# The transposed embeddings laid out slot by slot instead of sample by sample, in a DLRM interaction tower on one core

## Chip, cores and metric

One core of one Trainium2 chip. The metric is device time in microseconds of one execution of the kernel. Its engines are named as in the profile: PE (TensorE, with PEld for its weight loads), DVE (VectorE), ACT (ScalarE), POOL (GpSimd), SP (SyncE).

## The reference

For each of 512 samples, 27 embedding rows of 128 numbers are looked up in 27 tables, all pairs of the 27 are multiplied (a dot product each), and the 351 products with 16 dense numbers go through a tower of three layers. All in float32.

```python
e = jnp.stack([tbl_0[ids[:, 0]], ..., tbl_26[ids[:, 26]]], axis=1)   # 512 x 27 x 128
dot_products = jnp.einsum('bnd,bmd->bnm', e, e)
r, c = np.tril_indices(27, k=-1)
z = dot_products[:, c, r]
h = jnp.concatenate([z, dense_ctx], axis=1)                          # 512 x 367
h = jnp.maximum(h @ W_top1 + b_top1, 0.0)                            # 367 x 512
h = jnp.maximum(h @ W_top2 + b_top2, 0.0)                            # 512 x 256
y = h @ W_top3                                                       # 256 x 1
```

## The kernel before

**Tiling.** The 512 samples are T = 4 tiles of P = 128. The 128 numbers of an embedding lie on the 128 partitions, because the dot products contract over them. So every embedding has to stand transposed in a buffer, `embT` (line 107), with SLOT = 32 places for a sample's 27 embeddings; places 27 to 31 are zeroed (line 291).

**How the buffer is filled.** Nine tables of 1000 rows (ONEHOT) are looked up on PE as a product of the table with a one-hot matrix. DVE makes seven of the eight one-hot chunks (L238) and the low part of the table (L241), ACT makes the eighth chunk (L380, L383) and the high part (L391), PE multiplies (L456, L460), which gives one table's embeddings for all 512 samples in one PSUM bank of `fill`. ACT copies that bank into the buffer (L224). The other 18 tables (GATHERED) are gathered by POOL with one indirect DMA for each table and tile (L214, 72 in all), in groups of four tables and a last one of two (TG, five groups a tile). PE transposes each group into a bank of `fill` (L470), and ACT or DVE copies it into the buffer (L228). Both copies are in `take_fill` (lines 219 to 229).

**The products.** A tile's 128 samples are two units of 64. For each sample PE takes its 32 columns of the buffer as weights and its first 27 as moving data (`products`, L487). Four samples in a row, numbered `s`, write to the four quarters of the PSUM partitions, each with 32 of the array's columns. This text calls one MATMUL record of the trace a pass; a unit has 64 products and 128 passes, and the units are numbered 0 to 7. ACT and DVE merge a unit's products into `prod` (L351, L252), DVE transposes 32 x 32 blocks into `pairs` (L261), PE turns them (L501), ACT and DVE copy them to `pairsT` (L356, L266), and the three layers follow (L511, L523, L532) with their activations on ACT and DVE (L365, L373, L275, L283) and the output copy (L288).

**Order.** The order on every engine is written out by hand. PE first warms up (L538), then runs the list EARLY: nine one-hot lookups with the first eight groups of transposes between them (BETWEEN). After it come products(0,0), transposes(1,3), products(0,1), transposes(1,4), turn(0), products(1,0), the layers of tile 0, and so on tile by tile; before products(3,0) stand transposes(3,3) and (3,4). Products of a tile wait, at their first unit, for the last two fills to have been copied. All copies of EARLY are ACT's; later ones alternate between DVE and ACT. POOL's gathers for tile 3 wait until those of tile 0 have been transposed, since the gather buffer holds three tiles.

Of the kernel before, what the change touches and what calls it, by code (L numbers as in the profile page):

```python
# [6 lines left out]
B = 512  # L7
F = 27
# [3 lines left out]
P = 128  # L12
T = B // P
SLOT = 32
GS = P // SLOT
GROUPS = P // GS
UNIT = 16
GB = 4
# [17 lines left out]
X = len(ONEHOT)  # L36
# [29 lines left out]
def tower(nc, ids, ids_t, dense_t, tbls, w1, w2, cols, pick, y):  # L66
# [9 lines left out]
    def bank(i):  # L76
        return i % 4 if i < len(EARLY) else i % 2
# [4 lines left out]
    def taker(i):  # L82
        return "act" if i < len(EARLY) or i % 2 else "dve"

    def taken_of(i):
        return sum(taker(j) == taker(i) for j in range(i + 1))

    with ExitStack() as ctx:
        def sb(name, shape, dt=fp32):
            return ctx.enter_context(nc.sbuf_tensor(name, shape, dt))  # L90

        def pb(name, shape):
            return ctx.enter_context(nc.psum_tensor(name, shape, fp32))

        def sem(name):
            return ctx.enter_context(nc.semaphore(name))
# [7 lines left out]
        row_int = sb("row_int", [P, CH], i32)  # L104
        row_no = sb("row_no", [P, CH])
        emb = sb("emb", [P, EB, NG, D])
        embT = sb("embT", [P, T, P, SLOT])
        ident = sb("ident", [P, P])

        prod = sb("prod", [P, 2, GROUPS, MERGED])  # L110
# [15 lines left out]
        fill = pb("fill", [P, 4, BANK])  # L126
        gram = [pb(f"gram{i}", [P, BANK]) for i in range(GB)]
        gram = [g[:, 0:UNIT * F].rearrange("p (g j) -> p g j", j=F) for g in gram]
# [13 lines left out]
        zeros_ready = sem("zeros_ready")  # L142
# [76 lines left out]
        def take_fill(eng, copy, taken, what):  # L219

            i = FILL_NO[what]
            eng.wait_ge(filled, i + 1)
            if what[0] == "oh":
                copy(embT[:, :, :, what[1]].rearrange("p t b -> p (t b)"), fill[:, bank(i), :]).then_inc(taken, 1)  # L224
            else:
                _, t, g = what
                a, e = TG[g]
                copy(embT[:, t, :, X + a:X + e],  # L228
                     fill[:, bank(i), 0:(e - a) * P].rearrange("p (n b) -> p b n", b=P)).then_inc(taken, 1)

        @block.vector
        def _(dve):
# [11 lines left out]
            def take_transposes(*groups):  # L244
                for t, g in groups:
                    if taker(FILL_NO[("tr", t, g)]) == "dve":
                        take_fill(dve, nc.vector.tensor_copy, taken_v, ("tr", t, g))
# [40 lines left out]
                nc.vector.tensor_copy(y_sb[:, t * P:(t + 1) * P].rearrange("o (g s) -> o s g", s=GS),  # L288
                                      sums3.rearrange("o (s g) -> o s g", s=GS)).then_inc(y_ready, 1)

            nc.vector.memset(embT[:, :, :, F:SLOT].rearrange("p t b s -> p (t b) s"), 0.0).then_inc(zeros_ready, 1)
            dve.wait_ge(row_made, 1)
            nc.vector.tensor_copy(row_no[:], row_int[:]).then_inc(row_ready, 1)
            dve.wait_ge(row_ready, 1)
# [44 lines left out]
        def _(act):  # L339
            def take_transposes(*groups):  # L340
                for t, g in groups:
                    if taker(FILL_NO[("tr", t, g)]) == "act":
                        take_fill(act, nc.scalar.copy, taken_a, ("tr", t, g))
# [55 lines left out]
            for what in EARLY:  # L399
                take_fill(act, nc.scalar.copy, taken_a, what)  # L400
                if what[0] == "oh" and what[1] + 2 < X:
                    round_table(what[1] + 2)
                    onehot_chunk(what[1] + 2)
# [35 lines left out]
        def _(pe):  # L439
# [34 lines left out]
            def products(t, u):  # L474
                i = t * UNITS + u
                if u == 0:

                    last_fill = max(FILL_NO[("tr", t, NTG - 1)], FILL_NO[("oh", X - 1)])
                    for j in (last_fill - 1, last_fill):
                        pe.wait_ge(taken_v if taker(j) == "dve" else taken_a, taken_of(j))  # L480
                if i >= GB:

                    pe.wait_ge(merged, i - GB + 1)
                for g in range(UNIT):
                    for s in range(GS):
                        b = (u * UNIT + g) * GS + s
                        last = nc.tensor.matmul(gram[i % GB][SLOT * s:SLOT * (s + 1), g, :], embT[:, t, b, :],  # L487
                                                embT[:, t, b, 0:F], start=True, stop=True)
                last.then_inc(gram_ready, 1)

            def turn(t):
# [48 lines left out]
            for what in EARLY:  # L540
                if what[0] == "oh":
                    one_hot(what[1])
                else:
                    transposes(what[1], what[2])
            pe.wait_ge(zeros_ready, 1)
            products(0, 0)
            transposes(1, 3)
            products(0, 1)
            transposes(1, 4)
            pe.wait_ge(w_in, 80)  # L550
            turn(0)
            products(1, 0)
            layer1(0, (0, 1))
            layer1(0, (2, 3))
# [74 lines left out]
```

## Time and profile before

| | us |
|---|---|
| three runs | 181.49, 178.98, 178.2 |
| their median | 178.98 |
| the profiled execution | 177.67 |
| its span, first to last instruction | 175.8 |
| PE busy / PEld busy | 104.6 / 82.8 |
| POOL busy | 78.8 |
| DVE busy / ACT busy | 55.5 / 48.3 |
| mean granted TensorE clock | 0.806 |

Busy times are averages over the whole span; the kernel has stages with different limits, so the strips by slice and the timeline say more. A slice of the strips is 4.4 us. "issue" in a chain or in brackets is idle time of an engine that waited for nothing the profile shows. PE's durations overlap each other, since matmuls are pipelined.

### The profile page before, as it was taken

What the parts mean: (1) busy time and instruction counts of PE and PEld (TensorE: products, weight loads), DVE (VectorE), ACT (ScalarE), POOL (GpSimd) and SP (SyncE); (2) the same over time, 40 slices, a digit from 0 to 9 for tenths busy, and PEclk for the clock granted to TensorE, in tenths of its full rate; (3) what the DMA queues carried; (4) which work ended last, traced back from release to release, by engine and by line L of the source; (5) the groups of instructions that cost most, each with busy time, mean ns of one, the idle gap of its engine ahead of it and who ended that gap; (6) DMA issues with size and microseconds to landing.
All of it is one profiled execution on the core that took longest, in us unless ns stands there. A gap on an engine that the chain in (4) does not pass through costs nothing.

```text
span 175.8 us, 3411 instructions
## 1 busy us (share of the span) xinstructions
PE 104.6 (59%) x1486; PEld 82.8 (47%) x1486; DVE 55.5 (32%) x112; ACT 48.3 (27%) x84; POOL 78.8 (45%) x79
## 2 busy tenths in 40 slices
PE   6999999599982111100000002958969547972794
PEld 2448887487862110000000001748869437951693
DVE  5586978989700000000000000150343134123111
ACT  0581985999931000000000000311322111220010
POOL 4778877878777777777777730000000000000000
PEclk9999999999999555555555555599999996999579
DMA  4999999995121212121212110000000000000000
GB/s 76 278 256 267 346 273 247 240 241 122 34 60 49 60 45 60 45 60 45 60 45 60 51 38 0 4 4 4 4 0 0 4 4 4 0 4 4 0 4 0
DMA packets 6571, 13.59 MB, mean 77 GB/s; under 512 B 2422, under 2 KB 2998, under 8 KB 6428
## 3 DMA queue, kind: packets, MB, share of 16 engines
q1 hardware_dynamic: 4252, 8.64, 19.4%
q0 software_dynamic: 2304, 4.72, 9.9%
q8 instruction: 12, 0.20, 0.4%
q14 instruction: 3, 0.02, 0.0%
HBM read 13.36 MB, written 0.00 MB: 76 GB/s over the span
## 4 chain that ended last, share of the span: by engine, by line
issue 39%; PE 31%; POOL 21%; DVE 4%; DMA 3%; ACT 1%
POOL emb L214 21%; PE fill L511 10%; PE gram L487 10%; PE fill L523 4%; PE fill L470 3%; PE fill L501 2%; DVE pairs L261 2%; DMA emb<-tbl_dram,ids_sb 1%; DMA ids_sb<-ids_dram 1%; PE fill L532 1%; DVE prod L252 1%; DVE h L283 1%; ACT prod L351 1%; DVE pairsT L266 0%; ACT embT L228 0%
## 5 line engine op out<-in xcount | busy, mean ns | idle before, releaser
L214 POOL DMA_INDIRECT emb<-tbl_dram,ids_sb x72 | 78.0, 1084 | 23.2 <-issue 21.6
L487 PE MATMUL gram<-embT 128*32 128x27 f32 x1024 | 18.5, 202 | 56.0 <-issue 55.5
L487 PEld LDWEIGHTS gram<-embT 128*32 128x32 f32 x1024 | 14.9, 117 | 60.1 <-issue 59.1
L252 DVE COPY_PREDICATED prod<-pick_sb,gram 128x224 f32<-128x224 int32 x8 | 3.3, 407 | 79.7 <-ACT prod L351 79.7
L238 DVE TENSOR_SCALAR onehot<-ids_bc,row_no 125x512 fp32r<-125x512 int32 x63 | 26.0, 482 | 6.2 <-DMA ids_bc<-ids_t_dram 3.9
L351 ACT COPY prod<-gram 128x224 f32<-128x224 f32 x8 | 2.8, 345 | 72.6 <-PE gram L487 72.6
L511 PE MATMUL fill<-pairsT,w_sb 112*128 112x128 f32 (+1 forms) x128 | 18.3, 309 | 2.4 <-issue 1.6
L456 PE MATMUL fill<-onehot,high 125*128 125x512 f32 x72 | 19.2, 408 | 0.0
L511 PEld LDWEIGHTS fill<-pairsT,w_sb 112*128 112x128 f32 (+1 forms) x128 | 17.5, 222 | 3.3 <-issue 1.8
L460 PE MATMUL fill<-onehot,low 125*128 125x512 f32 x72 | 17.9, 390 | 0.0
L460 PEld LDWEIGHTS fill<-onehot,low 125*128 125x128 f32 x72 | 13.5, 188 | 2.9
L456 PEld LDWEIGHTS fill<-onehot,high 125*128 125x128 f32 x72 | 13.0, 188 | 3.2 <-issue 0.5
L470 PE MATMUL fill<-ident,emb 128*128 128x128 f32 x72 | 12.6, 299 | 2.5 <-DMA emb<-tbl_dram,ids_sb 2.4
L538 PE MATMUL fill<-ident 128*128 128x512 f32 x22 | 11.6, 692 | 1.6 <-POOL ident L204 1.6
L224 ACT COPY embT<-fill 128x512 f32<-128x512 f32 x9 | 10.0, 1112 | 7.8 <-PE fill L460 7.5
L241 DVE TENSOR_TENSOR low<-table,high 125x1024 fp32r<-125x1024 f32 x9 | 10.9, 1216 | 1.3 <-ACT high L391 1.3
L470 PEld LDWEIGHTS fill<-ident,emb 128*128 128x128 f32 x72 | 9.0, 151 | 4.9 <-issue 4.1
L391 ACT CAST high<-table 125x512 fp32r<-125x512 f32 x18 | 10.4, 628 | 2.7 <-DMA table<-tbl_dram 2.5
L228 ACT COPY embT<-fill 128x512 f32<-128x512 f32 (+1 forms) x14 | 9.4, 670 | 5.6 <-PE fill L470 5.5
L538 PEld LDWEIGHTS fill<-ident 128*128 128x128 f32 x22 | 4.9, 228 | 7.5 <-issue 5.9
L523 PE MATMUL fill<-h,w_sb 128*128 128x128 f32 x64 | 8.4, 279 | 0.0
L275 DVE TENSOR_SCALAR h<-fill,cols_sb 128x128 f32<-128x128 f32 x8 | 2.4, 347 | 18.5 <-PE fill L511 18.5
(25 smaller groups left out, 51.1 us busy)
## 6 DMA issues: line engine op xcount, KB each, us to landing
table<-tbl_dram SPq DMA_DIRECT2D x9, 448.0 KB
ids_bc<-ids_t_dram SPq DMA_DIRECT2D x9, 256.0 KB, 5.0
emb<-tbl_dram,ids_sb POOLq DMA_INDIRECT x72
w_sb<-w_dram SPq DMA_DIRECT2D x1, 1024.0 KB
w_sb<-w_dram SPq DMA_DIRECT2D x1, 512.0 KB
table<-tbl_dram SPq DMA_DIRECT2D x9, 52.0 KB
ids_sb<-ids_dram SPq DMA_DIRECT2D x1, 54.0 KB, 2.1
pairsT<-dense_t_dram SPq DMA_DIRECT2D x1, 32.0 KB
```

Of the source, the lines that this page charges most:

```text
L214: nc.gpsimd.indirect_dma_start(out=emb[:, t % EB, n, :], out_offset=None, in_=tbls[f], in_offset=bass.IndirectOffsetOnAxis(ap=ids_sb[:, t, ...
L224: copy(embT[:, :, :, what[1]].rearrange("p t b -> p (t b)"), fill[:, bank(i), :]).then_inc(taken, 1)
L238: nc.vector.tensor_scalar(onehot[:, n % 2, c, :], ids_bc[0:CR, n % NT, :], row_no[0:CR, c:c + 1], None, ALU.is_equal).then_inc(onehot_v, 1)
L241: nc.vector.tensor_tensor(low[:, n % 2, :], table[:, n % NT, :], high[:, n % 2, :].bitcast(fp32), ALU.subtract).then_inc(low_ready, 1)
L391: nc.scalar.copy(high[:, n % 2, a:a + half], table[:, n % NT, a:a + half]).then_inc(high_ready, 1)
L456: nc.tensor.matmul(fill[:, bank(i), :], high[:, n % 2, c * D:(c + 1) * D], onehot[:, n % 2, c, :], start=(c == 0), stop=False)
L460: last = nc.tensor.matmul(fill[:, bank(i), :], low[:, n % 2, c * D:(c + 1) * D], onehot[:, n % 2, c, :], start=False, stop=(c == CH - 1))
L470: last = nc.tensor.transpose(fill[:, bank(i), (n - a) * P:(n - a + 1) * P], emb[:, t % EB, n, :], ident[:])
L487: last = nc.tensor.matmul(gram[i % GB][SLOT * s:SLOT * (s + 1), g, :], embT[:, t, b, :], embT[:, t, b, 0:F], start=True, stop=True)
L511: last = nc.tensor.matmul(layer[m // 2][:, m % 2 * P:(m % 2 + 1) * P], w1_sb[0:rows, k, m * P:(m + 1) * P], pairsT[0:rows, t, k, :], start ...
L523: last = nc.tensor.matmul(layer[m2][:, 0:P], w2_sb[:, m, m2 * P:(m2 + 1) * P], h1[:, m, :], start=(m == 0), stop=(m == MC - 1))
L538: nc.tensor.matmul(fill[:, 3, :].rearrange("p (r c) -> p r c", r=4), ident[:], ident[:].unsqueeze(1).broadcast_to([P, 4, P]), start=True, ...
```

## The change

The buffer of transposed embeddings was indexed [partition, tile, sample, slot]; it becomes [partition, slot, sample], with all 512 samples of a slot in one run of 2 KB. The copy of a one-hot fill wrote 512 elements at steps of 128 bytes; it now writes one run of 512. The copy of a transposed group wrote, for each of 128 samples, up to four elements that lie together, reading PSUM at steps of 512 bytes; it now reads one run from PSUM and writes up to four runs of 128. The zeroing wrote 512 runs of five; it now writes one run of 2560. PE read a sample's slots side by side; it now reads them 2 KB apart, as weights and as moving data. Sizes, instruction counts, waits and the order on each engine stay; POOL's and SP's instructions are the same.

```diff
-        embT = sb("embT", [P, T, P, SLOT])
+        embT = sb("embT", [P, SLOT, B])
...
-                copy(embT[:, :, :, what[1]].rearrange("p t b -> p (t b)"), fill[:, bank(i), :]).then_inc(taken, 1)
+                copy(embT[:, what[1], :], fill[:, bank(i), :]).then_inc(taken, 1)
...
-                copy(embT[:, t, :, X + a:X + e],
-                     fill[:, bank(i), 0:(e - a) * P].rearrange("p (n b) -> p b n", b=P)).then_inc(taken, 1)
+                copy(embT[:, X + a:X + e, t * P:(t + 1) * P],
+                     fill[:, bank(i), 0:(e - a) * P].rearrange("p (n b) -> p n b", b=P)).then_inc(taken, 1)
...
-            nc.vector.memset(embT[:, :, :, F:SLOT].rearrange("p t b s -> p (t b) s"), 0.0).then_inc(zeros_ready, 1)
+            nc.vector.memset(embT[:, F:SLOT, :], 0.0).then_inc(zeros_ready, 1)
...
-                        b = (u * UNIT + g) * GS + s
-                        last = nc.tensor.matmul(gram[i % GB][SLOT * s:SLOT * (s + 1), g, :], embT[:, t, b, :],
-                                                embT[:, t, b, 0:F], start=True, stop=True)
+                        b = t * P + (u * UNIT + g) * GS + s
+                        last = nc.tensor.matmul(gram[i % GB][SLOT * s:SLOT * (s + 1), g, :], embT[:, :, b],
+                                                embT[:, 0:F, b], start=True, stop=True)
```

## Rows read from the trace of the kernel before

**Rows 1.** The page, chain that ended last, by engine.

```profile
issue 39%; PE 31%; POOL 21%; DVE 4%; DMA 3%; ACT 1%
```

**Rows 2.** The page, busy tenths in 40 slices, and the granted clock.

```profile
PE   6999999599982111100000002958969547972794
...
POOL 4778877878777777777777730000000000000000
PEclk9999999999999555555555555599999996999579
```

**Rows 3.** Timeline, stage 1: start us, us, engine, line, operation, count, idle before.

```profile
1.34 2.19 DVE L291 MEMSET embT<- 128x2560 f32 x1 [1.34 <-PEq L593]
...
51.51 1.04 ACT L224 COPY embT<-fill 128x512 f32<-128x512 f32 x1 [2.45 <-PE fill L460]
...
52.08 0.63 PE L470 MATMUL fill<-ident,emb 128*128 128x128 f32 x4 [0.61 <-DMA emb<-tbl_dram,ids_sb]
...
52.69 0.53 PE L487 MATMUL gram<-embT 128*32 128x27 f32 x39
```

**Rows 4.** Groups by line, POOL, 0 to 50 us, then 55 to 103 us.

```profile
L214 POOL DMA_INDIRECT emb<-tbl_dram,ids_sb x30 | 38.4, 1280 | 10.4 <-issue 8.8 <-DMA ids_sb<-ids_dram 1.6
...
L214 POOL DMA_INDIRECT emb<-tbl_dram,ids_sb x39 | 36.8, 944 | 11.9 <-issue 11.9
```

**Rows 5.** Windows: us, then busy (count) of PE, PEld, DVE, ACT, POOL, clock, DMA, GB/s.

```profile
80.00:103.00 23.00, 1.64 (x8) 1.16 (x9) 0.00 (x0) 0.00 (x0) 17.33 (x19) 0.50 0.18 52
```

**Rows 6.** Timeline, end of stage 2.

```profile
101.87 0.94 POOL L214 DMA_INDIRECT emb<-tbl_dram,ids_sb  x1 [0.30 <-issue]
...
109.88 0.79 PE L487 MATMUL gram<-embT 128*32 128x27 f32 x40 [1.15 <-issue]
```

**Rows 7.** Groups by line and shape, whole span: busy us, mean ns, idle before.

```profile
L391 ACT CAST high<-table 125x512 fp32r<-125x512 f32 x18 | 10.4, 628 | 2.7 <-DMA table<-tbl_dram 2.5 <-issue 0.2
L224 ACT COPY embT<-fill 128x512 f32<-128x512 f32 x9 | 10.0, 1112 | 7.8 <-PE fill L460 7.5 <-issue 0.2
...
L228 ACT COPY embT<-fill 128x512 f32<-128x512 f32 x12 | 8.6, 718 | 4.9 <-PE fill L470 4.8
...
L228 DVE COPY embT<-fill 128x512 f32<-128x512 f32 x4 | 2.8, 711 | 0.4 <-PE fill L470 0.4
...
L266 DVE COPY pairsT<-fill 112x256 f32<-112x256 f32 x4 | 1.7, 425 | 3.1 <-PE fill L501 3.1
```

**Rows 8.** Timeline, stage 3.

```profile
119.36 3.62 PE L511 MATMUL fill<-pairsT,w_sb 112*128 112x128 f32 x30 [1.60 <-issue]
...
139.96 0.25 PE L487 MATMUL gram<-embT 128*32 128x27 f32 x3 [1.97 <-issue]
...
143.78 0.27 PE L487 MATMUL gram<-embT 128*32 128x27 f32 x8 [1.84 <-issue]
...
155.79 0.71 ACT L228 COPY embT<-fill 128x512 f32<-128x512 f32 x1 [2.16 <-PE fill L470]
...
156.55 1.68 PE L487 MATMUL gram<-embT 128*32 128x27 f32 x173 [0.58 <-ACT embT L228]
...
160.16 0.91 PE L487 MATMUL gram<-embT 128*32 128x27 f32 x83 [1.93 <-issue]
```

**Rows 9.** Windows of L487 alone (units 1, 3): us, PE, PEld, clock, DMA, GB/s.

```profile
111.60:113.60 2.00, 1.93 (x128) 1.80 (x128) 0.50 0.00 0
...
125.10:126.45 1.35, 1.29 (x128) 1.18 (x128) 1.00 0.00 0
```

**Rows 10.** The page, DMA queues: packets, MB, share of 16 engines.

```profile
q8 instruction: 12, 0.20, 0.4%
```

**Rows 11.** The chain in order of time: start us, us, what.

```profile
49.43 2.38 DMA emb<-tbl_dram,ids_sb
```

**Rows 12.** Windows of all engines over L511 of tile 1 and of tile 3.

```profile
129.80:133.60 3.80, 3.76 (x33) 3.79 (x34) 0.00 (x0) 1.25 (x3) 0.00 (x0) 1.00 0.00 0
164.60:170.70 6.10, 6.07 (x34) 6.10 (x35) 0.00 (x0) 0.62 (x2) 0.00 (x0) 0.61 0.01 3
```

## The prediction

> **What bounds the kernel now.** I read the chain of waits first, then the engine strips, then the timeline around the long gap, then windows over one line. The chain [rows 1] has two parts that matter: 21% of the span is POOL's issuing of gathers (L214), and 39% is "issue", time in which an engine waited for nothing the profile shows. The strips [rows 2] say where that is: POOL is busy from the start to slice 24 of 40, and PE has its nines until about slice 12, then zeros and ones until slice 25, then work to the end. So there are three stages.
>
> Stage 1, 0 to 52.7 us. One-hot lookups on PE, DVE and ACT beside the gathers. At its end PE waits for a gather to land and starts the transposes of L470 at 52.08; the first product unit (L487) starts at 52.7 [rows 3]. POOL's gathers take 1280 ns each while DVE works and 944 ns when it doesn't [rows 4].
>
> Stage 2, 52.7 to 109.9 us. The first product unit, 128 passes long, does 39 passes in half a microsecond and then crawls: from 80 to 103 us it does 8 passes in 23 us [rows 5], one every 2.9 us. Nothing it waits for is seen, DVE and ACT are idle, and the granted clock is at 0.50 (1.2 of 2.4 GHz) from about 57 us on [rows 2], so after the crawl began. The crawl outlives the last gather (issued at 101.87) by some 7 us and ends in a burst at 109.88 [rows 6]. All four times of before lie within 177.67 and 181.49 us, so it is there each time. I can't name its cause; I only use that it began under the gathers and ended shortly after them.
>
> Stage 3, 109.9 to 175.8 us. A chain through PE with short hops to ACT and DVE: product units, stream transposes, three layers of the tower for four tiles.
>
> **The sum is made against the profiled execution**, 177.67 us with a span of 175.8, so 1.87 us lie outside the span. The median of the runs shown is 178.98. I keep the 1.87 and count changes within the span.
>
> **The change, part by part.** No instruction moves and none is added; forms change.
>
> Evictions of the one-hot fills (L224), 9 on ACT, all in stage 1. They now write each element on its own, 128 bytes apart, at 1112 ns; ACT's other pass over 512 elements per partition that writes one run, L391, takes 628 [rows 7]. Taking 628 for the new form saves 0.484 us each, 4.4 us of ACT time. What hides it: in stage 1 PE ends by waiting for gathers, whose pace ACT doesn't set, and the last L224 (51.51 to 52.55) holds up only the start of the first product unit [rows 3]. Taking 0.48 off it lets the unit start after the four transposes, some 0.3 us sooner, and then it runs into the crawl, whose end hangs on the gathers. Cost of this part at the end: 0. If the cover were gone it would be a gain of at most 0.3 us.
>
> Evictions of the transposes (L228), 14 on ACT, 6 on DVE. The full form writes runs of four and takes 718 ns on ACT, 711 on DVE; as whole runs I take 628 for ACT and leave DVE, since its run copy of 256 (L266) takes 425, of which two would be more than 711 [rows 7]. Nearly all lie beside PE's work. One is on the chain of stage 3, the ACT eviction from 155.79 to 156.50 for which the last tile's products wait [rows 8]. Gain: 0.1 us.
>
> The zeroing of the spare slots (L291), 2.19 us on DVE from 1.34 [rows 3]. As one run of 2560 elements it is at least no more steps. DVE's next needed work waits for the first ids, and the products that read these slots start at 52.7; the first eviction on ACT comes after several ACT passes. Counted at 0; were it to take 1 us more, it would delay the first one-hots by that, again hidden by the gathers.
>
> PE's reads (L487). This is the only part that lands on the end. Every product of a sample reads 32 columns as weights and 27 as moving data; before, they lie side by side, after, each is 2 KB from the next. Two records stand for each product (128 MATMUL records for a unit of 64 products [rows 9]), and four products go to four column groups of the array. A unit takes 1.29 us at clock 1.00 and 1.93 at 0.50, so a set of four passes takes 40 or 60 ns.
>
> No row shows PE reading at a stride, so I bound it. From below: no penalty, 0. From above: the nearest row is ACT's lone-element writing, (1112 - 628)/512 = 0.945 ns per element that stands alone [rows 7]. Moving data: 27 x 0.945 = 25.5 ns a pass; weights: 32 x 0.945 = 30.2 ns. The four column groups now work at once and weight loads run beside the passes (busy 1.18 beside 1.29 of the same 1.35 us [rows 9]). If that stays, a set grows by the larger, 30.2 ns, and a unit by 32 x 30.2 = 0.97 us. If weights and moving data add up, by 55.7 ns and 1.79 us. If in addition the four groups queue for one another, by 128 x 55.7 = 7.1 us. I take 0.97, the value in which what overlaps in the rows goes on overlapping.
>
> Here a page speaks against the change. The rows show a lone element costing ACT 0.945 ns more. The Trainium skill, "Advanced Engine Details and Errata", section SBUF Cachelines, says that SBUF lines are 16 bytes and that an access needs a second hit on its line for full speed; here every column would be on a line of its own. It gives no amount, and no run yet shows it for PE. Without such a rule the sum below would be -0.1, with it it is a loss of unknown size.
>
> How much of 0.97 per unit shows at the end? Stage 3 has gaps of 1.6 to 2.0 us in which PE waits for nothing shown, each once per one or two units: 1.60 in L511 after unit 2, 1.97 in unit 4, 1.84 in unit 5, 1.93 in units 6 and 7 [rows 8]. The instruction queue moved 12 packets, 0.20 MB, so some 16.7 KB each [rows 10]. I read the gaps as PE having used up its instructions sooner than the next piece arrives. Then the end of the gap is fixed by the arrival, and slower products before it only fill it. Unit by unit: the rest of unit 0 (40 of 128 passes) 10 x 30.2 ns = 0.30; unit 1 0.97; unit 2 0, in the gap of 1.60; unit 3 0.97 (what follows it there is a wait for DVE, which comes after the products); units 4 and 5 0; units 6 and 7: 173 passes stand before the gap and hide their 1.3 us in 1.93, the 83 behind it cost 21 x 30.2 ns = 0.64. Sum 2.88, less 0.1 for the eviction: +2.8. 177.67 + 2.8 = 180.4 us.
>
> On the gaps the page and the rows differ. The rows show the gaps. The Trainium skill, "Runtime: NRT & Kernel Launch", section Instruction fetch mechanics, says that instructions are refilled in 16 KiB blocks and that crossing one is mostly hidden; the size agrees with 16.7 KB, the hiding doesn't agree with gaps of 1.6 to 2.0 us. By the page there would be nothing to fill, and all units would pay: see rival 2.
>
> **Rivals.**
> 1. No penalty: PE reads 2 KB apart as fast as side by side. For it: the steps within a unit at clock 1.00 may be set by issuing, not by reading, since halving the clock adds only half (1.29 to 1.93). Against it: ACT's 1112. Time 177.67 - 0.1 = 177.6.
> 2. The gaps don't absorb: something else makes them, and each unit pays. Work: 0.30 + 7 x 0.97 = 7.1, less 0.1: 184.7 us.
> 3. Slower: weight loads and moving reads no longer overlap, 1.79 a unit. Place: L487 in stage 3. 0.56 + 1.79 + (1.79 - 1.60) + 1.79 + 0 + 0 + units 6 and 7 (43 sets add 2.40, 0.47 over the gap; 21 sets 1.17) = 5.97, less 0.1: 183.5 us. It decides from about 1.2 us a unit, where the result passes 2%. With the groups queueing as well, 7.1 a unit: 2.2 + 7.1 + 5.5 + 7.1 + 5.1 + 5.3 + 12.3 = 44.6, so 222 us. Against the latter: the rows show four groups at once, reading from four different places already.
> 4. The crawl of stage 2 goes or shortens, because slower products don't trigger what starts it. For it: it set in within half a microsecond of the densest run of PE so far. Against it: the products stay dense, and its end followed the gathers. If it goes wholly, the last gather is issued at 101.87 plus 0.94, lands some 2.4 us later (as an earlier one did [rows 11]), and the last tile's work from 155.09 to 175.8 follows: 102.8 + 2.4 + 20.7 + 1.87 = 127.8 us. Anything between that and the forecast is possible.
>
> **How the numbers follow.** Forecast (0.5 to 1.2 us a unit, gaps absorb) 0.41; rival 1 0.20; rival 2 0.10; rival 3 0.19, of it 0.06 for the heavy form; rival 4 0.10. Two per cent, about what a measurement of this kernel can tell from no change, is 3.6 us: from the profiled 177.67 the line is at 181.2, from the median at 182.6. Within 2%: rival 1 and four fifths of the forecast, 0.52 in all. Slower: rivals 2 and 3 and the rest, 0.38. Faster: rival 4, 0.10. Range: from a little under rival 1 to above rivals 2 and 3 in their light forms, 176.5 to 189; the heavy form and rival 4 are left out.
>
> **What would show it.** Right: L224 near 630 ns; unit 3 at about 2.3 us instead of 1.29; the gaps in units 4 to 7 shorter by what the products grew; the burst that ends stage 2 still near 110 us. Wrong: a unit at 1.3 us (rival 1), gaps as long as before behind slower units (rival 2), a unit at 3 us or more (rival 3), PE at full pace between 55 and 100 us (rival 4). A changed clock in stage 3 would spoil the sum too: L511's 32 passes took 3.8 us from 129.8 at clock 1.00 and 6.1 us from 164.6 at 0.61 [rows 12], so up to 2.3 us hang on how busy PE looks before it.

## The result, and the profile after

The changed kernel takes 187.96 us in the median of four runs (186.26 to 189.95), the kernel before 179.5 (178.2 to 181.49). The ratio is 1.047, with an interval of 1.034 to 1.059. The profiled execution took 188.05 us for a span of 186.0, that of before 177.67 for 175.8. Executions of one kernel differ by some per cent, and every ratio in this text is formed from its fast ones alone, while a time that stands alone is the median of all of them or, where that is said, one execution.

The groups by line and shape of the changed kernel, to be read against [rows 7] and the page's group for L252 of before (3.3 us busy, 407 ns in the mean):

```profile
L228 ACT COPY embT<-fill 128x512 f32<-128x512 f32 x12 | 9.8, 819 | 4.7 <-PE fill L470 4.6
...
L252 DVE COPY_PREDICATED prod<-pick_sb,gram 128x224 f32<-128x224 int32 x8 | 7.8, 976 | 80.8 <-ACT prod L351 80.8
...
L224 ACT COPY embT<-fill 128x512 f32<-128x512 f32 x9 | 5.3, 588 | 8.8 <-PE fill L460 8.8
```

The one-hot evictions (L224, the copies out of PSUM) went from 1112 to 588 ns, a little under the 628 I had taken, and the end of the kernel didn't come sooner for it. The transposed ones (L228 on ACT) should have become faster and are slower in the mean, and L252, which the change doesn't touch, takes 976 ns for 407. The means hide single long ones. The timeline of the changed kernel shows where they stand:

```profile
111.97 4.04 PE L487 MATMUL gram<-embT 128*32 128x27 f32 x128
112.07 2.41 ACT L228 COPY embT<-fill 128x512 f32<-128x512 f32 x1 [0.62 <-PE fill L470]
...
118.48 4.12 PE L487 MATMUL gram<-embT 128*32 128x27 f32 x128
118.59 1.90 ACT L356 COPY pairsT<-fill 112x256 f32<-112x256 f32 x1 [2.17 <-PE fill L501]
...
148.05 4.48 DVE L252 COPY_PREDICATED prod<-pick_sb,gram 128x224 f32<-128x224 int32 x1 [0.57 <-ACT prod L351]
...
148.12 4.43 PE L487 MATMUL gram<-embT 128*32 128x27 f32 x128
```

Copies of DVE and ACT that run beside a product unit last longer, by very different amounts: L228 2.41 us, L356 1.90 and L266 1.80 (for 0.37 and 0.42), L252 4.48, which ends with its unit, another L252 0.88. A copy that starts as a unit ends, as DVE's L228 at 152.44 with 0.63 us, is as fast as before or faster. In the kernel before no such row exists: its longest L252 is 0.42 us.

Windows of L487 alone in the changed kernel, units 1 and 3, and 6 with 7, to be read against [rows 9]:

```profile
111.90:116.10 4.20, 4.04 (x128) 3.93 (x128) 0.62 0.00 0
...
128.50:133.10 4.60, 4.46 (x128) 4.36 (x128) 1.00 0.02 4
...
163.90:171.10 7.20, 7.06 (x256) 6.98 (x256) 1.00 0.02 5
```

A unit takes 3.5 to 4.5 us where it took 1.3 to 1.9, and a higher clock no longer makes it shorter (4.04 us at a mean of 0.62 of 2.4 GHz, 4.46 at 1.00): reading sets the pace. At 1.00 alone the units differ, from 4.4 for units 3 to 5 down to 3.5 for 6 and 7; why is not shown. The gaps of [rows 8] inside units 4 to 7 are gone; the chain has L487 at 18% for 10% before. The crawl of stage 2 is unchanged: the burst that ends it starts at 109.69 us (109.88 before).

Reading both timelines side by side, the lateness of the changed kernel grows like this in stage 3 (start of each in before, in after, difference; L470 are transposes):

| | before | after | later by |
|---|---|---|---|
| transposes after unit 0 | 110.59 | 110.92 | 0.33 |
| L501 of tile 0, behind unit 1 | 115.50 | 117.93 | 2.43 |
| L470 behind unit 2 and L511 of tile 0 | 122.81 | 126.21 | 3.40 |
| unit 3 | 125.13 | 128.53 | 3.40 |
| unit 4, behind unit 3 and the layers of tile 1 | 136.61 | 143.22 | 6.61 |
| unit 5 | 140.72 | 148.12 | 7.40 |
| L501 of tile 2 | 145.92 | 154.42 | 8.50 |
| unit 6 | 156.55 | 163.99 | 7.44 |
| L501 of tile 3 | 162.93 | 172.90 | 9.97 |
| end of the span | 175.8 | 186.0 | 10.2 |

The step back from 8.50 to 7.44 is the clock. PE came to tile 2 at a granted 0.50 in before and at 1.00 in the changed kernel: L501 and the transposes behind it took 1.75 us and then 1.26, L511 4.36 and then 3.81. At the very end it goes the other way, L511 of tile 3 taking 6.05 us and then 6.45.

### The profile page after: what moved, and what is told of

Read it like the earlier page. It is cut to its first block, busy times and chain, and to the rows that moved or that the text cites. A ratio compares the mean times of both kernels' runs of the same rounds, so it can differ in the third digit from the quotient of the medians.

```text
span 186.0 us, 3411 instructions
## 1 busy us (share of the span) xinstructions
PE 123.6 (66%) x1486; PEld 102.5 (55%) x1486; DVE 66.0 (36%) x112; ACT 47.7 (26%) x84; POOL 78.8 (42%) x79
## 3 DMA queue, kind: packets, MB, share of 16 engines
q0 software_dynamic: 2304, 4.72, 9.5%
## 4 chain that ended last, share of the span: by engine, by line
PE 41%; issue 31%; POOL 14%; DVE 6%; DMA 6%; ACT 1%
PE gram L487 18%; POOL emb L214 14%; PE fill L511 10%; DMA emb<-tbl_dram,ids_sb 5%; PE fill L523 4%; DVE prod L252 3%; PE fill L470 2%; PE fill L456 2%; PE fill L460 2%; PE fill L501 2%; DVE pairs L261 2%; DMA ids_sb<-ids_dram 1%; PE fill L532 1%; DVE pairsT L266 1%; DVE h L283 1%
## 5 line engine op out<-in xcount | busy, mean ns | idle before, releaser
L487 PE MATMUL gram<-embT 128*32 128x27 f32 x1024 | 38.8, 286 | 48.1 <-issue 47.6
L487 PEld LDWEIGHTS gram<-embT 128*32 128x32 f32 x1024 | 35.7, 224 | 51.8 <-issue 50.8
L252 DVE COPY_PREDICATED prod<-pick_sb,gram 128x224 f32<-128x224 int32 x8 | 7.8, 976 | 80.8 <-ACT prod L351 80.8
L351 ACT COPY prod<-gram 128x224 f32<-128x224 f32 x8 | 3.4, 431 | 80.4 <-PE gram L487 80.4
L511 PE MATMUL fill<-pairsT,w_sb 112*128 112x128 f32 (+1 forms) x128 | 17.9, 306 | 1.0 <-DVE pairsT L266 1.0
L511 PEld LDWEIGHTS fill<-pairsT,w_sb 112*128 112x128 f32 (+1 forms) x128 | 17.2, 220 | 1.8 <-ACT pairsT L356 1.8
L470 PE MATMUL fill<-ident,emb 128*128 128x128 f32 x72 | 11.8, 286 | 1.6 <-DMA emb<-tbl_dram,ids_sb 1.6
L228 ACT COPY embT<-fill 128x512 f32<-128x512 f32 (+1 forms) x14 | 10.6, 754 | 5.4 <-PE fill L470 5.3
L470 PEld LDWEIGHTS fill<-ident,emb 128*128 128x128 f32 x72 | 8.7, 145 | 3.5 <-issue 2.4
L523 PEld LDWEIGHTS fill<-h,w_sb 128*128 128x128 f32 x64 | 7.7, 191 | 0.4 <-DVE h L275 0.4
```

The source lines that it names most:

```text
L228: copy(embT[:, X + a:X + e, t * P:(t + 1) * P], fill[:, bank(i), 0:(e - a) * P].rearrange("p (n b) -> p n b", b=P)).then_inc(taken, 1)
L252: nc.vector.copy_predicated(prod[:, t % 2, u * UNIT:(u + 1) * UNIT, :], pick_sb[:].unsqueeze(1).broadcast_to([P, UNIT, MERGED]), gram[i % ...
L470: last = nc.tensor.transpose(fill[:, bank(i), (n - a) * P:(n - a + 1) * P], emb[:, t % EB, n, :], ident[:])
L511: last = nc.tensor.matmul(layer[m // 2][:, m % 2 * P:(m % 2 + 1) * P], w1_sb[0:rows, k, m * P:(m + 1) * P], pairsT[0:rows, t, k, :], start ...
L523: last = nc.tensor.matmul(layer[m2][:, 0:P], w2_sb[:, m, m2 * P:(m2 + 1) * P], h1[:, m, :], start=(m == 0), stop=(m == MC - 1))
```

## The experiments

Three questions: is it the reading of PE, and which of the two reads; is it that elements lie alone or how far apart they lie; and where do the 8.5 us come from that one unit's growth of 0.97 us didn't give.

One finding overturned a premise and comes first. On the chips of all experiments but the last, the kernel before took 131 us, not 179: the crawl of stage 2 isn't there. So a comparison below is only between kernels of one chip. On those chips the times of one kernel also spread by 5 us and more (before, in eleven executions on one chip, from 125.89 to 134.16), so that a per cent is not to be had from them, and I read the traces first. No kernel whose PE reads are all in runs was measured on a chip with the crawl, so for the first chip the account by steps rests on its two traces.

**Which read.** All three kernels keep the changed evictions. Where a read is put into a run, it takes other numbers of the buffer than the product needs, as many as before; these kernels leave out the right products. The diffs are against the changed kernel's line L487.

```diff
 e1_moving_only
-embT[:, :, b], embT[:, 0:F, b]
+embT[:, (u * UNIT + g) % F, t * P + SLOT * s:t * P + SLOT * s + SLOT], embT[:, 0:F, b]
 e2_weights_only
+embT[:, :, b], embT[:, (u * UNIT + g) % F, t * P + SLOT * s:t * P + SLOT * s + F]
 e3_both_runs
+both of the above runs
```

> The changed kernel, but PE loads as weights 32 elements that lie in one run (of another place of the buffer, so the products are other products); the moving data stay 2 KB apart. In the changed kernel a product unit takes about 4.0 us at either clock, 128 passes. Theory A (weight loads and moving data each have a way of their own to the buffer, each taking one lone element every 0.83 ns, the four column groups queueing): 32 sets x 108 elements x 0.83 ns = 2.9 us a unit, time about 184 us. Theory B (one way for both, 236 lone elements a set at about 0.5 ns): 32 x 108 x 0.5 = 1.8 us a unit, time about 180 us. Theory C (only weight loads pay): 1.3 us a unit at full clock, time as before, 179 us.

> The mirror: weights 2 KB apart, the moving data 27 elements of one run of another place (other products). Theory A: 32 x 128 x 0.83 = 3.4 us a unit, time about 186 us, nearly all of the loss. Theory B: 32 x 128 x 0.5 = 2.1 us a unit, about 181 us. Theory C: as the changed kernel, 4.0 us and 188 us.

> Both reads of PE are runs of other places (other products), while the evictions and the zeroing keep their new form: the change without its reads. If all of the loss is PE's reading: units at 1.3 us (clock 1.00) and 1.9 us (0.50) again, the gaps of 1.6 to 2.0 us back, L252, L266 and L356 at their 0.4 us again, and 178 to 180 us: as before, since the 4.7 us that ACT saves lie behind the gathers. Rival: the evictions' gain shows, 175 us or less.

Measured: e1 131.87 us (ratio 0.984, 0.970 to 0.999), e2 134.4 (1.034, 1.020 to 1.048), e3 131.25 (1.001, 0.986 to 1.017), each against before at 130.86. The forecasts of total times for all three missed by about 50 us, for want of the crawl. By its ratio e1 isn't slower than before, although its units are. Its granted clock was 0.973 and 0.986 in its two fastest executions, that of before 0.906 and 0.907 in its own; that a clock held up gives back what the units cost fits this, and a1 below shows it in rows. The units tell the theories apart. The groups by line in the stretch of units 6 and 7, which no gather disturbs on any chip, 256 passes: e3, e1, e2 in this order.

```profile
L487 PE MATMUL gram<-embT 128*32 128x27 f32 x256 | 2.7, 198 | 2.6 <-issue 2.1 <-ACT embT L228 0.6
```

```profile
L487 PE MATMUL gram<-embT 128*32 128x27 f32 x256 | 5.0, 254 | 1.3 <-issue 0.7 <-ACT embT L228 0.6
```

```profile
L487 PE MATMUL gram<-embT 128*32 128x27 f32 x256 | 6.0, 245 | 0.6 <-ACT embT L228 0.6
```

So with both reads in runs PE is back at 2.7 us for two units, the gap is back, and the evictions' gain doesn't show, to within the 1.6% of the interval. Strided moving data alone make it 5.0, strided weights alone 6.0, both 7.2 (below). Theory C falls (moving data pay as well). Theory B's sums (3.6 and 4.2) are too small. Theory A's (5.8 and 6.8) are too large but nearer in form. The two reads overlap by about half: alone they add 2.3 and 3.3 us, together 4.5, halfway between the larger of the two and their sum of 5.6. The gap shrinks in step, 2.1, 0.7, none.

**The change itself and before on one chip without the crawl.**

> The changed kernel itself, beside the kernel before on one chip. On the chip of the first experiments the kernel before took 131 us instead of 179, with the first product unit at full pace (no crawl in stage 2). If that holds here: the crawl is no part of either kernel's own work, the gathers up to about 100 us hide units 0 to 5, only units 6 and 7 (2 x 2.3 us, less the gap of 1.9) and what they do to DVE's and ACT's work show, and the change costs 3 to 6 us: 134 to 137. If the crawl is back: 187 to 189 us.

> The kernel before, for its trace on this chip. If the crawl comes from the chip and not from the program: 131 us where a1_changed shows none, 179 where it shows one. Units 6 and 7, after the last gather, near 1.1 us each without the gap.

Measured: a1 135.39 us in the median of six, before 131.09 of eleven. The profiled executions are 133.61 and 131.27, spans 131.7 and 129.4, and they start unit 6 at the same time, to 0.03 us. Timeline of before (b1) from there:

```profile
109.89 1.68 PE L487 MATMUL gram<-embT 128*32 128x27 f32 x173 [0.58 <-ACT embT L228]
...
113.87 0.91 PE L487 MATMUL gram<-embT 128*32 128x27 f32 x83 [2.31 <-issue]
...
116.64 1.10 PE L501 MATMUL fill<-ident,pairs 128*112 128x128 f32 x4 [1.86 <-DVE pairs L261]
```

And of the changed kernel (a1):

```profile
109.86 7.21 PE L487 MATMUL gram<-embT 128*32 128x27 f32 x256 [0.56 <-ACT embT L228]
...
118.95 1.10 PE L501 MATMUL fill<-ident,pairs 128*112 128x128 f32 x4 [1.87 <-DVE pairs L261]
```

This is the cleanest reading of the study. The 256 passes take 1.68 + 0.91 = 2.59 us plus a gap of 2.31 before, and 7.21 without a gap after. Of the 4.62 us that PE lost, the gap swallowed 2.31, and the other 2.31 are the whole difference of the spans (131.7 - 129.4 = 2.3). The last tile's layers behind them take as long in both (L511 5.93 and 5.96 us).

That unit 6 starts at the same time is not the gathers' doing. The last gather for which PE waits stands before L470 at 62.28 us in b1 and at 57.08 in a1; from there on the chain runs through PE in both. Units 0 and 1 are made up for in these waits and in an earlier start (L501 of tile 0 at 63.61 and 63.67). Units 2 to 5 put the changed kernel behind, by 1.34 us at L501 of tile 1 and by 1.13 at that of tile 2, and each time the layers make it up, because they run at a higher clock. L511 of tiles 1 and 2 in b1, at a mean granted clock of 0.69 and 0.84:

```profile
81.31 5.44 PE L511 MATMUL fill<-pairsT,w_sb 128*128 128x128 f32 x32 [0.17 <-DVE pairsT L266]
...
100.92 4.45 PE L511 MATMUL fill<-pairsT,w_sb 128*128 128x128 f32 x32
```

In a1, both at 1.00:

```profile
82.65 3.81 PE L511 MATMUL fill<-pairsT,w_sb 128*128 128x128 f32 x32 [0.17 <-DVE pairsT L266]
...
101.56 3.81 PE L511 MATMUL fill<-pairsT,w_sb 128*128 128x128 f32 x32 [0.17 <-DVE pairsT L266]
```

In a1 PE has no gap inside a unit and is busy without a break through each; in b1 it idles inside units 4, 5 and 7. The mean granted clock was 0.936 to 0.962 in all six executions of a1 and 0.883 to 0.918 in the eleven of before. So slow units pay back a part of their price on these chips, through the clock and the gaps.

How large the loss is there is less sure than how it comes about. The two profiled executions differ by 2.3 us, the medians by 4.3, and the fastest executions (125.89 and 133.61) by 7.7; no trace of an execution of before near 126 us exists to account for the rest.

**Alone, or too far apart.** The pitch between a sample's columns was varied by padding (e4: `B + 4`; e6: `B + 16`; f2: `B + 64`), by grouping four samples (e5) and by stacking the slots within a tile (f1):

```diff
-        embT = sb("embT", [P, SLOT, B])
+        embT = sb("embT", [P, SLOT, B + 4])
+        embT = sb("embT", [P, B // GS, SLOT, GS])
+        embT = sb("embT", [P, SLOT, B + 16])
+        embT = sb("embT", [P, T, SLOT, P])
+        embT = sb("embT", [P, SLOT, B + 64])
```

> The changed kernel with each slot's run padded by four elements, so that a sample's columns lie 2064 bytes apart instead of 2048. If the pitch is slow because all 32 addresses fall on one bank of the memory: units near 1.3 us, time near 179 us. If each lone element costs whatever the pitch: units of 4 us and 188 us as with the change.

> Another layout: for every four samples the slots follow one another, and the four samples' values of a slot lie together in 16 bytes. Evictions write runs of four, PE reads at steps of 16 bytes. If each lone element costs PE time whatever the pitch: as e4_pitch_2064, units near 2.0 us and a loss of 2% against before. If it is the reach of the addresses (32 elements over 64 KB) that costs: units at 1.1 us and the time of before or up to 1 us less. L224 should lie between 590 and 1112 ns.

> The changed kernel with a pitch of 2112 bytes, 132 lines of 16 bytes, where 2064 was 129 lines and 2048 is 128. If lines go round a number of banks that is a power of two, 2112 reaches a quarter of them at most where 2064 reaches all: units between 2.0 us (2064) and 4.0 us (2048), and L252 above 0.41 us in part. If 2048 is slow for another reason than a common bank: 2.0 us as with 2064.

> Slots one under the other within each tile of 128 samples: a sample's columns lie 512 bytes apart, 32 lines of 16 bytes. If PE's reads are slow by how few banks their lines reach, and 2048 (3.3 to 4.1 us a unit) and 512 are both multiples of the whole round: units again at 3.3 us or more, L252 above 0.8 us in the mean, time as a1_changed against its before (+3%). If only pitches above 512 collide: between 2.0 and 2.4 us a unit, as 16, 2064 and 2112 bytes had, and the time within 1% of before.

> Pitch 2304 bytes, 144 lines, that is 9 x 16, so a sixteenth of a power-of-two round of lines, where 2112 was 33 x 4 and took 2.3 us a unit, 2064 was odd and took 2.0, 2048 is 128 and took 3.3 to 4.1. If banks explain it: above 2.3 and up to 4 us. If not: 2.0 to 2.1 us.

Units 6 and 7 by the same view, and the longest L252 of each:

| kernel | pitch, bytes | in lines of 16 | busy, 256 passes, us | longest L252, us |
|---|---|---|---|---|
| b1_before | 4 (side by side) | | 2.6 | 0.42 |
| e5_quads | 16 | 1 | 4.5 | 0.43 |
| e4_pitch_2064 | 2064 | 129 | 4.5 | 0.44 |
| e6_pitch_2112 | 2112 | 132 | 4.9 | 0.48 |
| f1_pitch_512 | 512 | 32 | 6.8 | 4.67 |
| f2_pitch_2304 | 2304 | 144 | 6.9 | 4.58 |
| a1_changed | 2048 | 128 | 7.2 | 3.23 |

e4 came out between its two cases (1.3 and 4.0 us a unit) with 2.25. The units of e5, e6, f1 and f2 came out as the first case of each had them. The groups by line of e4 and of f2 in that stretch:

```profile
L487 PE MATMUL gram<-embT 128*32 128x27 f32 x256 | 4.5, 226 | 1.3 <-issue 0.7 <-ACT embT L228 0.6
```

```profile
L487 PE MATMUL gram<-embT 128*32 128x27 f32 x256 | 6.9, 270 | 0.6 <-ACT embT L228 0.6
```

Two costs come apart. That each element stands alone costs 4.5 - 2.6 = 1.9 us for two units, 0.95 a unit, at 16 bytes as at 2064: not how far, but whether. On top of it the pitches of 512, 2048 and 2304 bytes cost another 1.2 us a unit or more (6.8 to 7.2), and they alone hold up DVE and ACT; 2112 costs 0.2. With one of the two reads at 2048 bytes, the other in runs, the longest L252 is 1.17 us (e1) and 1.60 (e2). The distance isn't what counts, since 512 is slow and 2112 isn't. All slow pitches are multiples of 256 bytes, the quick ones aren't. That fits memory in banks taken in turn by lines of 16 bytes, with 16 lines to the round, so that a sample's 32 columns all fall into one, where a copy of DVE or ACT must queue as well. This is inferred from the pitches of the table and not shown: a round of 8 lines would fit too, and no odd multiple of 128 bytes was run to tell the two apart. The Trainium skill has the first cost, in "Advanced Engine Details and Errata", section SBUF Cachelines (16-byte lines, a second hit on one wanted for full speed), and the runs agree, with 0.95 us a unit. The Trainium skill's page "SBUF — State Buffer", section Who interferes with whom, says that PE and ACT never wait on anyone; the row above of ACT's L228 with 2.41 us, where the same copy beside no unit takes 0.59, disagrees, and the measurement decides.

The times: e4 133.08 us (ratio 1.024, 1.013 to 1.034, against 130.86), e5 132.37 against 131.09, e6 129.13 in one run, f1 135.97 and f2 135.57 (one run) against 131.19. By these medians f1 and f2 lose 4 to 5 us, as a1 did (4.3); f1's fastest execution (131.37) is 2.6 us above the fastest of before (128.8), so the size is loose. The others are not apart from before by these runs, e4 excepted. None is shown to beat before, and e3 says why one hardly would: the evictions that the layout makes faster save nothing that shows, even when PE's reads cost nothing.

e5 has one more thing to tell. Its evictions write runs of only four elements, and L224 takes 587 ns, L228 on ACT 581, as in e3 with runs of 512 and 128 (589 and 579). Runs of four are enough for ACT here. Before, L228 wrote runs of up to four as well and took 718, so its gain isn't in the length of the runs written, as the prediction had it. What is left is that it read PSUM at steps of 512 bytes, and that its runs began 4 bytes behind a multiple of 16 bytes (at slots 9, 13, 17 and 21) where those of e5 begin on one; no run tells the two apart.

**Where the units lie.** f3 is the kernel before, g1 the changed one, with one wait more:

```diff
+            pe.wait_ge(gathered[T - 1][NTG - 1], 32)
             pe.wait_ge(zeros_ready, 1)
             products(0, 0)
```

> The kernel before, with one more wait: PE starts the first product unit only when the last gather has landed, about 105 us. On the two chips seen since, units 0 to 5, which run beside the gathers, take 1.6 to 2.0 us of issuing with pauses of 0.2 to 0.3 us, units 6 and 7 take 1.1 without. If the gathers make these pauses (and, on the first chip, the crawl): all units at 1.1 us at full clock, none with a pause but for the gaps of about 2 us, and a time of 105 + 66 + 2 = 173 us, on any chip. If the pauses belong to the place in the program: units 0 to 5 at 1.6 to 2.0 us again.

> The changed kernel with the wait of f3_after_gathers, so that on any chip all eight units stand behind the last gather, as they nearly do on the first chip because of the crawl. f3_after_gathers took 178.5 us. If the 8.5 us of loss on the first chip are PE's slow units where nothing hides them (with their effect on DVE and ACT), and the 2 to 3 us on the other chips the same loss with units 0 to 5 hidden beside the gathers: 8 to 12 us more than f3, 187 to 191. Rival: the first chip's loss belongs to the crawl: 181 to 183 us.

f3 took 178.52 us on a chip where before took 131.19: pushing all units behind the gathers gives about the first chip's time without any crawl. I had expected 173; its stage 3 is 69.8 us long (106.8 to 176.6) instead of 65.9. Of the 3.9 more, 1.1 is that f3 has all of unit 0 in it and before only its last 40 passes; L511 of tiles 2 and 3 take 5.81 and 6.67 us instead of 4.36 and 6.05, at a lower clock; and the gaps are 1.84 to 2.26 us instead of 1.60 to 1.97. Timeline of f3 at the first unit:

```profile
106.79 1.93 PE L487 MATMUL gram<-embT 128*32 128x27 f32 x128 [51.57 <-DMA emb<-tbl_dram,ids_sb]
```

Units beside the gathers and behind them differ even on a chip without the crawl. In b1 the passes of unit 0 start over 1.64 us, of unit 2 over 1.98 and of unit 3 over 1.90, with two or three pauses of 0.16 to 0.28 us in each; in f3 unit 3 starts its passes over 1.10 us at the same clock as unit 3 of b1 (1.00), with no pause. Of f3's units one, unit 1, has such a pause (0.30 us from one start to the next), with nothing left to gather. So the pauses come mostly beside the gathers and cost a few tenths of a microsecond; that the gathers make them is likely and not shown.

g1 took 189.58 us in the median of four (186.43 to 191.47), 11.1 more than f3, as the first theory had it (8 to 12), though on another chip and with some 3.5 us of crawl in it that f3 doesn't have. By chance it ran on a chip that has the crawl: before took 178.87 there, and g1 against it is 1.054 (1.031 to 1.078). Its trace shows the crawl again, with nothing left to gather:

```profile
105.20 1.90 PE L487 MATMUL gram<-embT 128*32 128x27 f32 x41 [50.81 <-DMA emb<-tbl_dram,ids_sb]
107.67 0.21 PE L487 MATMUL gram<-embT 128*32 128x27 f32 x1 [0.57 <-issue]
...
109.77 0.21 PE L487 MATMUL gram<-embT 128*32 128x27 f32 x1 [1.13 <-issue]
```

It lasts from 107.1 to 110.48 us instead of 57 us, steps by the same 0.70 or 1.4 us, and ends. So gathers aren't needed to start it, and what makes it end is open. The three chips on which before took 131 us ran the same program as the first chip and this one (which may be one and the same) at 179, so what decides on the crawl is in the chip or its surroundings, not in the kernel alone.

## Why the prediction was right, and where not

The forecast was slower by 2.7 us, a size it called within noise, with a range of 176.5 to 189; measured were 187.96, near the upper end, and a loss clear of noise. The direction and the place of the loss, PE's reads in stage 3, were forecast. That the time lies within the range is luck: the range reaches that far only for rivals 2 and 3, and neither's mechanism is what happened. By steps:

- **Evictions.** Right: L224 at 588 ns for 628 forecast, and no gain; e3 agrees with the cover, to within its interval. The gain of 0.1 us on the one L228 in the chain came (0.71 to 0.59).
- **The zeroing at 0.** Right: L291 takes 2192 ns in both forms.
- **A lone element costs PE what it costs ACT, 0.97 us a unit.** The number came out for what it described, 0.95 (e4 and e5, units 6 and 7), though by an analogy between two engines that nothing had borne out. But the step that failed is this same term of the sum: the forecast took the price of an element standing alone for the whole price of a pitch of 2 KB. The pitch costs another 1.35 us a unit at its quietest ((7.2 - 4.5)/2), and a unit grew by 2.1 to 3.2, not by 0.97. In the sum that is unit 1 +2.1 for 0.97, unit 3 +3.2 for 0.97, and what stood at 0 because a gap covers it came through: unit 2 +1.0, units 4 and 5 +0.8 and +1.1; units 6 and 7 +2.5 for 0.64. With +0.3 for the rest of unit 0, as forecast, that is 11.0, of which the clock of tile 2 gave back 1.1.
- **The gaps absorb slower products.** Right, and shown by a1 and b1: 4.62 us more of products, 2.31 of them in the gap. They absorb up to their length and no more. In the eight traces that have a gap in unit 7 it comes after the same 173 passes and ends 3.6 to 4.0 us after unit 6 began, whether these passes took 1.7 us (before, b1, e3, f3) or 3.0 to 3.2 (e1, e4, e5, e6), so its end doesn't hang on how fast PE works. Rival 2 falls. That the gaps are instructions on their way stays an inference; the Trainium skill's page "Runtime: NRT & Kernel Launch", section Instruction fetch mechanics, would have the crossing mostly hidden, and gaps of up to 2.3 us stand against it in every trace in which PE's reads are runs.
- **Weight loads and moving data go on overlapping.** By about half at 2 KB: 5.0 and 6.0 us alone and 7.2 together, against 2.7 with both in runs. Rival 3's mechanism, that they add up in full, is refuted, while its size a unit (1.79) was nearer to the truth than mine and its sign, a unit of 3 us or more, did come.
- **No effect of PE on DVE and ACT.** Not considered at all. Copies that meet a unit last up to 4.48 us in the changed kernel. In the table of lateness it doesn't show by itself, since the copies are done when the unit is; it might show where one is needed sooner.
- **Rival 1** (no penalty) is refuted by the units of every strided kernel. **Rival 4** (the crawl goes) didn't happen on the first chip, and the argument for its chance, that slower products don't trigger it, is idle: the crawl started with slow products too.
- **The clock.** The prediction named it as what could spoil the sum, and left it out of the sum. It gave back 1.1 us on the first chip, and in a1, together with the gaps, all that units 2 to 5 cost.
- **"So it is there each time."** Wrong as a premise. Four times on one chip say nothing of another. Where it is missing, the same change loses 2.3 us by the profiled executions and 4.3 by the medians, instead of 10.4 and 8.5.

## What to carry to other kernels

A buffer that PE reads many times and others write once should lie as PE reads it: in the reads of a product, elements that stand alone cost about a microsecond per 128 small passes here, and the pitches that are multiples of 256 bytes (512, 2048, 2304) cost that again and more, and slowed DVE and ACT beside it; four elements of padding took the second cost away. Before a saving is counted ask what the engine is waiting for, since ACT's 4.7 us were worth nothing; before a loss is counted look for a gap behind it, since 2.3 of 4.6 us vanished in one, and at the granted clock of what follows, since L511 took 3.81 us behind slow units where it took 5.44 and 4.45 behind quick ones.

## What the runs showed of the hardware that I hadn't expected

- PE's reads at 512, 2048 and 2304 bytes delay other engines: DVE's 0.41 us copy (L252) took up to 4.67 us, ACT's 0.59 us copy (L228) 2.41, and 3.26 in a1. POOL's gathers, 0.95 us each in stage 2 of before, took up to 2.29 in a1 and 2.32 in f2. At 2064 and 2112 bytes the longest L252 was 0.44 and 0.48, and no gather behind 55 us took over 0.95.
- At a pitch of 2048 bytes a higher granted clock didn't shorten a unit (4.04 us at a mean of 0.62, 4.46 at 1.00).
- On the first chip and on that of g1 PE, in its first dense run of small products, falls to one instruction per 0.7 or 1.4 us, for 57 us beside the gathers and for 3.4 us behind them; on three others it doesn't, and only pauses for 0.16 to 0.28 us in b1. The kernel takes 179 us on the former and 131 on the latter. What differs between the chips stays open.
